# Setup and Gram matrix in one block, first convolution input prepared there, z2 statistics gathered in two sets

## The reference, cut to what matters

```
ternarize(w): a = |w|; delta = 0.7 * mean(a); mask = a > delta
              alpha = sum(a * mask) / max(sum(mask), 1); return alpha * sign(w) * mask
out = relu(batchnorm(conv(x, ternarize(w1)), g1, b1))                    # 1x1, 96 -> 576
out = relu(batchnorm(conv(out, ternarize(w2), pad=1, groups=576), ...))  # depthwise 3x3: its result is "z2"
out = batchnorm(conv(out, ternarize(w3)), g3, b3);  x = out + x          # 1x1, 576 -> 96
batchnorm: mean and variance over all 32 images and all pixels
```

## Time and profile before

| | |
|---|---|
| median of 3 runs | 5704.41 us (5702.91 to 5705.4) |
| the profiled execution | 5686.37 us, its span 5684.6 us |
| mean granted TensorE clock | 0.934 |
| TensorE / VectorE / ScalarE / GpSimd busy | 92% / 67% / 60% / 37% of the span |
| setup block | from the start to about 76.3 us |
| Gram block | to about 351.1 us |
| convolution block | to about 2057.4 us |
| everything else | to 5684.6 us |

### The profile page before, as it was taken

One profiled execution on the slowest core, in us unless ns is written; L12 is line 12 of the kernel. 1 busy time (PEld: TensorE's weight loads), 2 busy tenths in 40 slices (PEclk: granted clock), 3 DMA queues, 4 the chain that ended last, 5 costly groups with the idle time before them and its releaser, 6 DMA issues.

```text
span 5684.6 us, 146458 instructions
## 1 busy us (share of the span) xinstructions
PE 5213.9 (92%) x59604; PEld 3484.0 (61%) x59604; DVE 3813.3 (67%) x6799; ACT 3411.5 (60%) x5674; POOL 2111.4 (37%) x1092
## 2 busy tenths in 40 slices
PE   4979999999999969999589999999999999999996
PEld 4966666666666634444366676666676766766663
DVE  2036666666666666767257777877777777777775
ACT  1445555555555558888256666666666666666653
POOL 0037777777777736666211111111111111111111
PEclk9989999999999989999689899999988998999986
DMA  3646666666666669999456656656556565565551
GB/s 79 158 115 163 171 168 161 171 170 169 171 163 168 153 254 414 415 411 416 132 148 171 163 152 177 165 158 174 155 159 164 159 165 164 152 177 160 163 133 45
DMA packets 493783, 1041.28 MB, mean 183 GB/s; under 512 B 176464, under 2 KB 345232, under 8 KB 460112
## 3 DMA queue, kind: packets, MB, share of 16 engines
q1 hardware_dynamic: 493120, 1031.92, 62.9%
HBM read 552.39 MB, written 478.94 MB: 181 GB/s over the span
## 4 chain that ended last, share of the span: by engine, by line
PE 40%; ACT 3%; DVE 3%; DMA 2%; issue 2%; SPq 0%; POOL 0%; DVEq 0%; POOLq 0%; ACTq 0%
PE bank_w L1359 6%; PE bank_s L1368 5%; PE bank_l L1269 4%; PE bank_x L1314 4%; PE bank_c L1322 3%; PE bank_o L1339 3%; PE bank_c L1323 3%; PE bank_o L1350 2%; PE bank_c L1329 2%; PE bank_l L1296 2%; ACT h L1432 2%; PE bank_x L1311 1%; PE bank_l L1257 1%; PE bank_l L1263 1%; DMA c_scratch<-cc 1%
## 5 line engine op out<-in xcount | busy, mean ns | idle before, releaser
L720 POOL TENSOR_TENSOR hlo<-h,hhi 128x1682 f16<-128x1682 f32 x288 | 977.2, 3393 | 449.2 <-DVE hhi L751 449.2
L735 DVE BATCH_NORM_STATS2 stats<-z 128x6 f32<-128x392 f32 x1152 | 597.3, 561 | 519.0 <-ACT z L672 509.1
L682 ACT ACTIVATE h<-c1ps,s 128x1512 f32<-128x1512 f32 x288 | 465.1, 1615 | 697.2 <-PE c1ps L598 697.2
L1551 POOL TENSOR_TENSOR y<-zin,x_tok 96x448 f32<-96x448 f32 x224 | 263.4, 1176 | 1341.7 <-ACT zin L1507 1340.1
L619 PE MATMUL dwps<-hhi,taps 64*64 64x392 f16 x13824 | 689.0, 330 | 3.7 <-issue 3.6
L619 PE MATMUL dwps<-hlo,taps 64*64 64x392 f16 x13824 | 681.3, 327 | 1.9 <-issue 1.8
L1559 POOL TENSOR_TENSOR onat<-tb,o 96x448 f32<-96x448 f32 x224 | 240.9, 1075 | 1113.9 <-DVE o L1618 1113.9
L870 ACT ACTIVATE z2m<-z2m,s 128x784 f32<-128x784 f32 x512 | 489.6, 1029 | 107.0 <-DMA z2m<-z_scratch 106.6
L894 POOL TENSOR_TENSOR h_split<-z2m,h_split 128x1568 f16<-128x1568 f32 x128 | 405.0, 3164 | 300.8 <-DVE h_split L933 300.8
L619 PEld LDWEIGHTS dwps<-hlo,taps 64*64 64x64 f16 x13824 | 406.1, 106 | 179.5 <-issue 3.3
L619 PEld LDWEIGHTS dwps<-hhi,taps 64*64 64x64 f16 x13824 | 381.8, 106 | 176.6 <-issue 6.3
(11 more groups left out here) (223 smaller groups left out, 10695.1 us busy)
## 6 DMA issues: line engine op xcount, KB each, us to landing
z_scratch<-z SPq DMA_DIRECT2D x1152, 196.0 KB, 3.3
z2m<-z_scratch SPq DMA_DIRECT2D x64, 1960.0 KB, 15.7
z2m<-z_scratch SPq DMA_DIRECT2D x64, 1568.0 KB, 11.4
a_scratch<-a SPq DMA_DIRECT2D x224, 384.0 KB, 2.8
bt<-a_scratch SPq DMA_DIRECT2D x96, 672.0 KB, 8.9
c_scratch<-cc SPq DMA_DIRECT2D x128, 336.0 KB, 4.3
d<-c_scratch SPq DMA_DIRECT2D x128, 336.0 KB, 4.6
xa<-in_x_dram SPq DMA_DIRECT2D x32, 1176.0 KB, 7.4
```

What stands on the lines that cost most here:

```text
L682: nc.scalar.activation(to, src, ACT.Relu, bias=s1[:, 1, u:u + 1], scale=s1[:, 0, u:u + 1]).then_inc(h_ready, 1)
L720: nc.gpsimd.tensor_tensor(to, h, hi, ALU.subtract).then_inc(lo_ready, 1)
L735: nc.vector.bn_stats(stats[:, i, v, at:at + 6], z2[:, v % 3, g, r, :]).then_inc(s_stat, 1)
```

## The change

Four things are done.

1. Setup and Gram become one block. SP loads `ident` first, then the images, and behind each of the images 1 to 8 up to ten of the other 72 small loads. TensorE starts on the Gram work at once and gets the six totals and the 20 turns between the Gram groups, at fixed places: the totals at steps 90, 94, ..., 110 and the turns at steps 130 to 149, counting eight steps per image. VectorE does the whole setup chain beside it; the absolute values are now its own instructions (three more), and ScalarE's two square roots stand after image 11's copies.
2. Each of the two `gps` banks accumulates over all its 16 images and is read out once, at the end; the 32 additions by VectorE become a copy and an addition.
3. Loading `xin`, the first image's `xhi` and `xlo`, clearing `h32` and building the taps move from the convolution block into the combined block.
4. The z2 statistics of pairs 0 to 12 are gathered by 18 `bn_aggr` spread over pairs 13 and 14, those of pairs 13 to 15 by 18 smaller ones, 12 of them within pair 15 and six behind it; three small instructions mix the two sets.

```diff
+        pre = keep.enter_context(ExitStack())
+        xin = sb("xin", [C, 2, TOK], ctx=pre)
...
-            loads.append((ident[:, :], ident_d))
...
-            @block.sync
-            def _(sp):
-                for dst, src in loads:
-                    sp.dma_start(dst, src, allow_slow_non_contiguous=True).then_inc(s_ld, 16)
-                sp.wait_ge(s_ld, ALL)
...
+            def setup_tensor(pe, step):
+                k, n = step - 90, step - 130
+                if 0 <= k < 24 and k % 4 == 0:
+                    totals_tensor(pe, k // 4)
+                if 0 <= n < len(turns):
+                    turn_tensor(pe, n)
...
+                nc.vector.tensor_scalar(abn[:, :, 3:4], abn[:, :, 3:4], EPS, None, ALU.add).then_inc(s_svar, 1)
+                nc.vector.tensor_scalar(abn2[:, 3:4], abn2[:, 3:4], EPS, None, ALU.add).then_inc(s_svar, 1)
                 for k, n in enumerate((C * PL, 9 * PL, C * PL)):
                     f = n // C
-                    dve.wait_ge(s_abs, k + 1)
+                    link(nc.vector.scalar_tensor_tensor(out=flat_abs[:, 0:f], in0=flat[k][:, :], scalar=-1.0,
+                                                        in1=flat[k][:, :], op0=ALU.mult, op1=ALU.max))
...
-        st = ExitStack()
-        with st:
             xa = sb("xa", [C, 2, TOK], ctx=st)
...
             def _(sp):
+                sp.dma_start(ident[:, :], ident_d).then_inc(s_ident, 16)
+                for n in range(NB):
+                    if n >= 2:
+                        sp.wait_ge(turned, (n - 1) * NG)
+                    sp.dma_start(xa[:, n % 2, :], x[n]).then_inc(ld[n % 2], 16)
+                    if n >= 1:
+                        for dst, src in loads[10 * n - 10:10 * n]:
+                            sp.dma_start(dst, src, allow_slow_non_contiguous=True).then_inc(s_ld, 16)
                 for m in range(2):
-                    sp.dma_start(xa[:, m, :], x[m]).then_inc(ld[m], 16)
-                for i in range(1, NP):
-                    for m in range(2):
-                        sp.wait_ge(turned, (i - 1) * (2 * NG) + NG * (m + 1))
-                        sp.dma_start(xa[:, m, :], x[2 * i + m]).then_inc(ld[m], 16)
+                    sp.dma_start(xin[:, m, :], x[m]).then_inc(ldx[m], 16)
+                sp.wait_ge(s_ld, ALL)
...
                         if g >= 1:
-                            if g == 1:
-                                wait_count(pe, added, i * 2 + m - 1)
                             pe.wait_ge(copied, n + g)
...
-                                                       start=(g == 1 and k == 0), stop=(g == NG and k == 3))
+                                                       start=(i == 0 and g == 1 and k == 0),
+                                                       stop=(i == NP - 1 and g == NG and k == 3))
                             ins.then_inc(xt_used, 1)
+                        setup_tensor(pe, (2 * i + m) * (NG + 1) + g)
...
+                    if i == min(5, NP - 1):
+                        for k, v in enumerate((abn[:, :, 3:4], abn2[:, 3:4])):
+                            act.wait_ge(s_svar, k + 1)
+                            nc.scalar.activation(v, v, ACT.Sqrt).then_inc(s_sstd, 1)
+                for c in range(NCH):
+                    xhi_scalar(act, 0, 0, c)
...
+            @block.gpsimd
+            def _(pool):
+                for c in range(NCH):
+                    xlo_pool(pool, 0, 0, c)
...
+                nc.vector.memset(xT[:, :, :, C:C + 1], 1.0).then_inc(s_init, 1)
+                setup_vector(dve)
...
+                nc.vector.memset(h32[:, :, :, :], 0.0).then_inc(s_zero, 1)
...
+                dve.wait_ge(xt_used, NB * NG)
+                link(nc.vector.tensor_copy(gacc[:, :], gps[0][:, 0:C + 1]))
+                nc.vector.tensor_tensor(gacc[:, :], gacc[:, :], gps[1][:, 0:C + 1], ALU.add).then_inc(s_gacc, 1)
...
+            LAST = 3
+            EARLY = NP - LAST
+            def gather_early(dve, u, g):
+                dve.wait_ge(s_stat, EARLY * NV * 4)
+                nc.vector.bn_aggr(mvs[:, 0, u, g, :], stats[:, 0:EARLY, u:u + UN + 1:UN, 12 * g:12 * g + 12]
+                                  ).then_inc(s_aggr, 1)
...
+            def gather(dve, i, v):
+                n = (i - EARLY) * NV + v - 4
+                if 0 <= n < 2 * NV - 8:
+                    for u, g in gathered[n * NV // (2 * NV - 8):(n + 1) * NV // (2 * NV - 8)]:
+                        gather_early(dve, u, g)
+                u = v - UN - 3
+                if i == NP - 1 and u >= 0:
+                    for g in range(2):
+                        gather_late(dve, u, g)
...
-                dve.wait_ge(s_stat, NN * 4)
-                for u in range(UN):
+                for u in range(NV - UN - 3, UN):
                     for g in range(2):
-                        link(nc.vector.bn_aggr(mv[:, u, g, :], stats[:, :, u:u + UN + 1:UN, 12 * g:12 * g + 12]))
...
+                nc.vector.scalar_tensor_tensor(out=both, in0=old, scalar=EARLY / LAST, in1=new, op0=ALU.mult,
+                                               op1=ALU.add).then_inc(s_mix, 1)
```

More of the change, by code:

```diff
@@ L271, in _ @@
-            @block.tensor
-            def _(pe):
-                for k in range(3):
-                    pe.wait_ge(s_rows, 2 * k + 1)
-                    nc.tensor.matmul(ps[0][:, 0:1], ones[:, :], rows[:, 0:1], start=True, stop=True).then_inc(s_tot, 1)
-                    pe.wait_ge(s_rows, 2 * k + 2)
-                    nc.tensor.matmul(ps[1][:, 0:2], ones[:, :], rows[:, 1:3], start=True, stop=True).then_inc(s_tot, 1)
-                pe.wait_ge(s_tin, 1)
-                for n, (src, p, f, dst) in enumerate(turns):
-                    if n >= 2:
-                        pe.wait_ge(s_tfree, n - 1)
-                    nc.tensor.transpose(ps[2 + n % 2][0:f, 0:p], src, ident[0:p, 0:p]).then_inc(s_tout, 1)
@@ L284, in _, with totals_tensor, turn_tensor @@
-            @block.vector
-            def _(dve):
+            def totals_tensor(pe, k):
+                pe.wait_ge(s_rows, k + 1)
+                bank, cols = (ps[0], rows[:, 0:1]) if k % 2 == 0 else (ps[1], rows[:, 1:3])
+                nc.tensor.matmul(bank[:, 0:1 + k % 2], ones[:, :], cols, start=True, stop=True).then_inc(s_tot, 1)
+            def turn_tensor(pe, n):
+                src, p, f, dst = turns[n]
+                if n == 0:
+                    pe.wait_ge(s_tin, 1)
+                if n >= 2:
+                    pe.wait_ge(s_tfree, n - 1)
+                nc.tensor.transpose(ps[2 + n % 2][0:f, 0:p], src, ident[0:p, 0:p]).then_inc(s_tout, 1)
@@ new lines, in _ @@
+                one = lane[:, 0:32].unsqueeze(1).broadcast_to([128, UN * 3, 32])
+                for da in range(2):
+                    for y in range(2):
+                        to = taps[:, :, da, :, y, :]
+                        v = wv[:, da, y, :, :].unsqueeze(3).broadcast_to([128, UN, 3, 32])
+                        nc.vector.tensor_tensor(to, one.rearrange("p (u x) c -> p u x c", u=UN), v,
+                                                ALU.mult).then_inc(s_taps, 1)
+                dve.wait_ge(xt_used, NB * NG)
@@ L570, in _ @@
             def _(sp):
-                for m in range(2):
-                    sp.dma_start(xin[:, m, :], x[m]).then_inc(ldx[m], 16)
                 conv_sync(sp, 0, False, True)
```

165 lines of the change are left out of this document (71 added, 94 removed).

## The result

The first four runs of the changed kernel took 5568.2 us in the median (5558.96 to 5592.77), four of the kernel before beside them 5704.9 us (5702.91 to 5722.83). The ratio is 0.9757, with a 95% interval of 0.9725 to 0.9790: the kernel is 2.4% faster. 5586 us was forecast, with a range from 5577 to 5602. The profiled execution took 5558.96 us, its span is 5557.2 us at a mean granted clock of 0.936; that of before had 5684.6 and 0.934. Between these two executions the gain is 127.4 us.

A forecast was written before the change was run, and what follows sets the result against it. TensorE was taken to bound the Gram and convolution loops, issue of small loads the setup. Gains 75.6 + 17.4 + 31.5 = 124.5 less 6.2 back, net 118.3 us: 5704.4 - 118.3 = 5586 us, range 5577 to 5602.

The forecast's parts named there:

- three seams: Setup before Gram work, Gram block to first convolution matmul, gathering behind the last statistics: gains of 124.5 us together.
- the first: Rival: small loads hold up the Gram images, 16 to 24 us come back, about 5605 us; chance 0.10.
- Start: Setup: TensorE's first Gram work moves from 85.13 to 9.5 us, a gain of 75.6 us.
- Gram stage: Gram loop: turns 3.0, totals 1.5, table load with square roots 0.4 and small loads 1.0 us come back.
- The stall of 1.7 us: Before image 12: by the skill's page, ScalarE's table switch with its drain would cost 1.7 us instead of 0.4.
- Chain: After the last Gram multiplication: the last addition becomes a copy and an addition, 0.3 us back.
- They hide behind other work: Gram block: first image's loading and splitting, clearing and taps fit into idle time; GpSimd's splitting has some 5 us left over.
- Seam: Gram block's end to first convolution matmul: TensorE starts at 352.0 instead of 369.45 us, a gain of 17.4.
- the third rival: Convolution's first steps: TensorE's clock already at its upper level, by estimate 1.3 us a step, 5582 us; no separate chance.
- Statistics: Behind the last statistics: six small gatherings and one mixing instruction instead of 34.6 us, a gain of 31.5.
- VectorE was no bound: Rival, pairs 13 and 14: gathering makes VectorE the bound, 18 us come back, 5604 us; chance 0.05.
- the fourth: Rival, Gram images: small loads go one at a time, 136 us back, 5722 us; chance 0.01.

The follow-up runs named there:

- a1: The changed kernel run again unaltered, five runs: 5580.88 us, ratio 0.9769 to the kernel before.
- e10: Changed kernel with GpSimd's `xlo` held until `prodd` is made, useless matmuls in the norm's chain and an early ScalarE `Copy`: 5577.1 us, ratio to before 0.9789.
- e8: Changed kernel with GpSimd's splitting into `xlo` held back until VectorE has written `prodd`: 5581.58 us.
- e5: Changed kernel with the small loads in batches of twenty behind an image instead of ten: 5603.25 us in one run.
- e7: Changed kernel with each of the 18 early gathering instructions in pairs 13 and 14 done twice: 5593.59 us.
- e4: Kernel before with only the first image's loading and splitting, clearing and taps moved into the Gram block: 5697.6 us, ratio 0.9976.

## Why the prediction missed its range, step by step

Direction, places and mechanism held: three seams, gains where they were forecast, and of the rivals only a trace of the first. The sum was 118.3 us; measured up to the second norm are 126.0 in the first pair of profiles and 2057.4 - 1934.3 = 123.1 with the second of after.

- **Start**, forecast 75.6: 76.2 (8.95 instead of 9.5).
- **Gram stage**, forecast 5.9 back: 1.9 and 3.0. Of the terms this one was sized worst, by 2.9 to 4.0 us. The turns cost 1.5 us instead of 3.0. The totals cost 0.9 instead of 1.5: images 11 to 13, from 97.37 to 121.43, took 24.06 us against 23.16. The small loads took 0.2 us in after and 0.7 in a1 instead of 1.0, at images 5 and 8 above all. The square roots with their table load, ahead of image 12, are at most 0.1 of these 0.9, instead of 0.4 by themselves: image 12 took 8.06 us (105.37 to 113.43), images 11 and 13, with two totals each as well, 8.00. The stall of 1.7 us that the prediction set beside this term didn't come: the load at 104.49 ends 0.01 us before the square roots.
- **Not foreseen in the Gram stage** were two things that nearly cancel. TensorE idles 1.28 us for the table load in front of the first copy, and the first image took 11.01 us against 9.87 before. How much of that is the load is known to about a microsecond: the same image took 10.97 to 12.40 us in the other kernels with the merged block and 10.51 in e10, where the load is out of the way. And an image without a neighbour takes 7.72 us instead of the 7.78 of before (102.72 to 110.50): over some 30 images 1.8 us less. What went there is one wait in TensorE's list for an addition, which the forecast had put at nothing because VectorE sat idle. The addition it asks for, of the image two back, was long done, so it seems to be the wait itself that costs. The kernel before bears it out, though no run isolates it: its image 1 is the only one but the first without that wait, and took 102.72 - 95.00 = 7.72 us. TensorE idles 0.25 us ahead of its first Gram matmul, and 0.34 at image 2:

```profile
95.00 0.83 PE L415 MATMUL tps<-ident,xa 96*112 96x96 f32 x8
...
96.08 0.92 PE L423 MATMUL gps<-xT 112*96 112x97 f32 x8 [0.25 <-ACT xT L449]
...
103.89 0.89 PE L423 MATMUL gps<-xT 112*96 112x97 f32 x8 [0.34 <-ACT xT L449]
```

- **Chain**, 0.3 back: 1.3, of which 1.4 is the conflict of e8, less 0.4 to 0.5 for products that began before the clock fell. "They hide behind other work" was counted as free for VectorE too; that step failed, at the price of 2.0 us (e8).
- **Seam**, 17.4: 17.7. TensorE at its lower clock in the first steps: so it was, and the third rival did not come about.
- **Convolution**, 0: 3.0 and 1.0 gained. Kernels with the same loop took 1643 to 1651 us; where the clock's rise falls differs between them, and no run settles more.
- **Statistics**, 31.5: 32.3. Six small ones took 2.16 us instead of 2.9. The large ones took 1546 ns (1560 forecast) and were hidden.
- **The rivals.** The first came true in tenths: the flights of images got longer by up to some 2 us while the small loads went out, and where image 8 was late, it was by its flight. e5 shows that at twenty in a batch it comes true in full, and there SP's issue decides, which passes its limit first. VectorE was no bound; e7 shows it is close. One load at a time, the fourth, would have put the images of the first 80 us some 26 us apart; they are 7.7 to 8.2.

The terms differ from the forecast by 7.7 us (4.8 in the second profile), all small and all but the chain on one side. That alone puts the time at 5578 to 5581, inside the range. **The step that failed is the last one**: "its seams should be the same, so I subtract the same from the median", with a range built of the terms' bounds alone. The kernel before, in 48 runs of this study, took 5671.6 to 5729.7 us, median 5704.6; the changed one, in nine, 5558.96 to 5592.77, median 5573.3. The mean granted clock goes with it: before took 5671.6 at 0.936, 5700 at 0.931 and 5729.7 at 0.924; after 5559 at 0.936, 5573 at 0.934 and 5592.8 at 0.930, some 4 to 6 us for each 0.001. A median over four such runs moves by several us by itself, and that wasn't in the range. Of the 18 us between forecast and measurement 5 to 8 are thus the terms, the Gram stage first among them, 5 are the draw of the first four runs against all nine, and the last 5 to 8 stay open: with all runs the gain is 131 us, in the stages up to the second norm 123 to 126, and nine runs that spread over 34 us can hardly tell the two apart. Open is also what decides the clock in the rest of the kernel. That the five runs of a1, with a median of 5580.88, fall inside the range is luck as much as the miss of the first four.

## What to carry to other kernels

Setup work belongs beside the first stage that doesn't need it, as long as its loads are issued in batches that fit between two of the stage's own; count SP's issue time (about half a microsecond a load) beside the bytes. A median over all 32 images hides what happened to the seven that the loads touched. Work that fills an idle engine at a seam can still slow another: look for GpSimd beside VectorE. And a range must hold the run-to-run spread of the time as well as the bounds of the terms, above all where the sum is known to a few us.

## What was unexpected of the hardware

- A VectorE copy of 96x576 takes 0.46 us alone and 1.15 to 1.17 beside GpSimd's splitting, or again 0.46 where it gets in ahead of a piece (e4); an instruction on 128x9 took 0.17 alone and 0.50 or 0.96.
- A transpose put into a full matmul stream costs 0.075 to 0.08 us, though two neighbours of the setup started 0.24 apart; a one-column product costs 0.15 there and 0.42 in the chain.
- ScalarE's switch of tables for the square roots cost the Gram loop under 0.1 us; for the first load of the kernel TensorE idled 1.28 us.
- An image with one more wait in TensorE's list, for something long done, took 7.78 us, one without 7.72; that the wait is the cause is argued.
- Identical code in the rest of the kernel took 2948 to 2985 us, at mean granted clocks from 0.936 to 0.928.
